# Attention phase of a fused layer kernel: the value product over four query tiles at once, and two output tiles before a batch's last half

## The chip, the cores and the metric

The kernel runs on one core of a Trainium2 chip. The metric is the device time of one execution in microseconds. All data is float32.

## What is computed

The reference is two transformer-like layers one after the other: a state-space block with a top-2 mixture of experts, then causal attention with a second mixture of experts. The change touches only the attention of the second layer:

```python
qkv = jnp.einsum('bte,fe->btf', x, Wqkv).reshape(B, T, H, 3 * D)
q, k, v = ...                       # each B, H, T, D
q, k = q + pe, k + pe
scores = jnp.einsum('bhtd,bhsd->bhts', q, k) / sqrt(D)
probs = softmax(where(causal, scores, -inf), axis=-1)
attn = jnp.einsum('bhts,bhsd->bhtd', probs, v)
out = jnp.einsum('btf,ef->bte', attn.reshape(B, T, H * D), Wo)
...
x = x + ga * out
```

Here B = 4 sequences ("batches") of T = 1024 tokens, 8 heads of D = 128, model width 256. After it the result is normalised again with other modulation rows (`cb`, `sb`), and a router picks two of 16 experts for each token.

## The kernel before

`phase_attention` is one block in which every engine has its own program, and semaphores tie them together. A batch is `HEADS * TPB` = 64 steps, numbered n, for 8 heads h = n // 8 and 8 query tiles i = n % 8 of 128 tokens. For one query tile i only the keys up to it count, that is i + 1 tiles of 128.

**TensorE** does in step n, in this order: `score(n)` (queries stationary, keys moving, up to 1024 columns into one of two score banks), `project` of one of six pieces of the next head's queries, keys and values (in six of the eight steps, `PROJECT`), `turn(n - 2)` (i + 1 transposes of 128x128 of the probabilities of two steps ago into `pt_ps`), and `weigh(n - 3)` (L1794 to L1804). In steps 32, 36, 40 and 44 (`R_PAIR`) `turn_pair` comes ahead of `weigh` and `logits` behind it: router work of the previous batch. Step 52 (`RANK`) has `count_before`, and step 53 waits for the ranks. Steps 56 to 63 (`TURN`) transpose the next batch's normalised rows (`turn_rows`). Behind the loop come eight `output(t)`, 8 matmuls of 256 columns each.

`weigh(n)` is the product with the values: for each key tile j up to i one matmul with the value tile j stationary and one transposed 128x128 block of probabilities moving, i + 1 matmuls of 128 columns, summed in `o_ps`. Each float32 matmul of the source stands as two weight loads and two matmuls in the trace.

**ScalarE** does in step n: `copy_turned(n - 2)` (L1901, out of `pt_ps` into `pt`), then `exponential(n)`; `copy_pair` between the two in the steps of `R_PAIR`, and at step 26 (`ROOT`) the square roots of the norms.

**VectorE** does in step n: `keep(n - 4)` (L2109, a copy of 128x128 out of `o_ps` into `attn`, which waits for `weigh(n - 4)`), then side work, then `maximum(n)` (mask, row maximum, bias), `normalise(n - 1)` (reciprocal and scale, L2101 and L2104), and `take_piece` (L2081, L2085) of the piece projected in the step. Side work is `stats` for the next batch in steps 1, 4, ..., 22 (`ADD`), `variance` at step 24 (once for the next batch and once for the router's norm of the previous; batches 0 and 3 have one of them), route rows in steps 29 to 43, `pick` in 46 and 48, weights, ranks and slots in 52 to 54, and `normalise_rows` of the next batch in 53 to 60. After the loop it adds each output tile to `x` (L2146 to L2150).

So the places that matter in a head are `score` -> `maximum` -> `exponential` -> `normalise` -> `turn` -> `copy_turned` -> `weigh` -> `keep`. `score(n)` waits for `exponential(n - 2)`; `turn(n)` waits for `normalise(n)`.

**SyncE** loads at the start, in this order, the first batch of `x` and `more`, the modulation rows, `mods2` (all modulation rows of the router's norm, 1 MB), `gate_w`, `pos`, `w_o`, then the next batches; it stores the four output batches after its last load. TensorE begins with waits for `w_qkv`, `w_o` and both loads that count in `route_in` (`mods2` and `gate_w`), ahead of its first `turn_rows`.

Of the kernel before, what the change touches and what calls it, by code (L numbers as in the profile page):

```python
# [7 lines left out]
ALU = mybir.AluOpType  # L8
# [1557 lines left out]
def phase_attention(nc, d, sh):  # L1566
# [10 lines left out]
    PIECES = 3 * CPB  # L1577
    with ExitStack() as ctx:
# [12 lines left out]
        pt = sb("pt", [P, 2, TPB, P])  # L1591
# [3 lines left out]
        more = sb("more", [P, TPB, E])  # L1595
# [4 lines left out]
        o_ps = ps("o_ps", [P, P])  # L1600
        qk_ps = ps("qk_ps", [P, CH])
        mods2 = sb("mods2", [P, 2, B, E])
# [11 lines left out]
        names = ("x_in summed route_in stats2_in stats2_chain var2_ready std2_ready rstd2_ready r_half_ready r_row_ready r_turned_done "  # L1614
# [9 lines left out]
        ADD = tuple(1 + 3 * j for j in range(TPB))  # L1624
        VAR, ROOT, INVERT = ADD[-1] + 2, ADD[-1] + 4, ADD[-1] + 6

# [14 lines left out]
        def _(sp):  # L1641
# [8 lines left out]
            sp.dma_start(w_o[:], d["woT"].rearrange("(h p) e -> p h e", p=P)).then_inc(S["w_o_in"], 16)  # L1650
            for b in range(1, B):
# [3 lines left out]
                sp.dma_start(more[:], d["more0"][b * T:(b + 1) * T, :].rearrange("(j p) e -> p j e", p=P)).then_inc(S["x_in"], 16)  # L1655
                sp.wait_ge(S["x_in"], b * 32)
            for b in range(B):
                sp.wait_ge(S["chain"], (b + 1) * TPB)
                rows_out = d["out"][b * T:(b + 1) * T].rearrange("(j p) e -> p j e", p=P)
                sp.dma_start(rows_out, sh.x[:, b * TPB:(b + 1) * TPB]).then_inc(S["x_stored"], 16)  # L1660
# [48 lines left out]
        def _(pe):  # L1709
# [39 lines left out]
            pe.wait_ge(S["route_in"], 32)  # L1749
# [4 lines left out]
            def batch(b, first_batch, last_batch):  # L1754
# [63 lines left out]
                for n in range(N + 3):  # L1818
# [19 lines left out]
                    if n >= 3:  # L1838
                        weigh(n - 3)
# [415 lines left out]
```

## Time and profile before

| | us |
|---|---|
| median of 3 runs | 3036.36 |
| lowest, highest run | 3032.16, 3041.62 |
| the profiled execution's own time | 3031.74 |
| its span, first to last instruction | 3030.0 |
| attention phase, first to last TensorE work | 1478.8 to about 2669 |
| TensorE busy in the span | 2651.9 (88%) |
| VectorE busy in the span | 2219.6 (73%) |

The profile is of one execution. "Busy" of TensorE counts matmuls up to their modelled ends, which overlap: the next matmul starts before the last has ended. Distances from start to start tell how long a stretch of matmuls takes. A span of steps is found by its first `score` of 128 columns (tile 0 of a head).

### The profile page before, as it was taken

How to read it: one execution, taken by the hardware profiler on the slowest of the kernel's cores; microseconds unless marked ns; L12 is line 12 of the kernel's file. 1: busy time of each engine (PE TensorE's matmuls, PEld its weight loads, DVE VectorE, ACT ScalarE, POOL GpSimd, SP SyncE). 2: the span in 40 equal slices, each digit the busy share in tenths (PEclk: the TensorE clock that was granted, in tenths of full speed). 3: DMA queues.
4: the chain of work that ended last, by engine and by line, in shares of the span. 5: the costliest groups of instructions: out<-in, count | busy, mean ns of one | idle time of the engine just before them, and what ended most of it. 6: DMA issues, size and time to landing. Idle time of an engine off the chain costs nothing. (4 is left out here: it accounts for less than half of the span.)

```text
span 3030.0 us, 38485 instructions
## 1 busy us (share of the span) xinstructions
PE 2651.9 (88%) x11504; PEld 1751.7 (58%) x11505; DVE 2219.6 (73%) x4787; ACT 1129.1 (37%) x2199; POOL 1233.9 (41%) x518
## 2 busy tenths in 40 slices
PE   5788888888887859999499999999999999839998
PEld 3233333333333647777277777776777777727776
DVE  4999999999999557777476757766776667525554
ACT  4557566566564201111133414332433233201111
POOL 1798898998999025665100000020002000224444
PEclk8899999999998659999799999999999999959999
DMA  4545545555555343333400000000000000125554
GB/s 156 170 150 181 173 159 178 171 161 175 178 163 177 122 138 60 59 60 58 132 29 1 1 1 29 1 30 15 1 1 29 15 1 1 43 89 126 125 125 71
DMA packets 150092, 269.22 MB, mean 89 GB/s; under 512 B 18300, under 2 KB 106412, under 8 KB 149292
## 3 DMA queue, kind: packets, MB, share of 16 engines
q1 hardware_dynamic: 120972, 227.12, 23.5%
q0 software_dynamic: 28416, 38.05, 7.6%
q10 hardware_dynamic: 544, 2.10, 0.2%
q8 instruction: 80, 1.31, 0.2%
q14 instruction: 80, 0.66, 0.1%
HBM read 209.65 MB, written 57.56 MB: 88 GB/s over the span
## 5 line engine op out<-in xcount | busy, mean ns | idle before, releaser
L692 POOL TENSOR_TENSOR dbx<-u,b_all 128x2048 f32<-128x2048 f32 x128 | 577.8, 4528 | 104.2 <-DVE u L766 49.6
L1690 POOL DMA_INDIRECT slots<-at_r_rows,slot_of x64 | 63.8, 997 | 1170.9 <-DVE slot_of L2035 1152.6
L432 PE MATMUL y_ps<-hc,ident 128*128 128x512 f32 x768 | 406.2, 647 | 115.9 <-DVE hc L846 114.8
L585 ACT ACTIVATE da_ps<-delta,a_neg 128x512 f32<-128x512 f32 x512 | 346.2, 689 | 319.1 <-DVE hc L846 312.7
L1901 ACT COPY at_pt<-at_pt_ps 128x512 f32<-128x512 f32 (+3 forms) x384 | 171.4, 481 | 512.3 <-PE at_pt_ps L1791 511.1
L432 PEld LDWEIGHTS y_ps<-hc,ident 128*128 128x128 f32 x768 | 140.4, 199 | 341.4 <-DVE hc L846 242.6
L1803 PE MATMUL at_o_ps<-at_pt,at_v 128*128 128x128 f32 x2304 | 299.8, 275 | 1.9 <-DVE at_attn L2109 1.9
L1780 PE MATMUL at_s_ps<-at_qk 128*128 128x512 f32 (+3 forms) x768 | 291.4, 489 | 5.0 <-DVE at_v L2085 3.1
L1803 PEld LDWEIGHTS at_o_ps<-at_pt,at_v 128*128 128x128 f32 x2304 | 277.9, 192 | 9.7 <-issue 9.7
L1891 ACT ACTIVATE at_probs<-at_s_ps,at_small 128x128 f32<-128x128 f32 (+7 forms) x256 | 191.6, 748 | 207.3 <-DVE at_small L2096 206.9
L846 DVE TENSOR_TENSOR hc<-da_ps,c_all 128x512 f32<-128x512 f32 x384 | 257.2, 671 | 0.1
L829 DVE TENSOR_TENSOR_SCAN da_ps<-da_ps,state,dbx 128x512 f32<-128x512 f32 x192 | 243.2, 1276 | 6.7 <-ACT da_ps L585 6.7
L829 DVE TENSOR_TENSOR_SCAN da_ps<-da_ps,dbx 128x512 f32<-128x512 f32 x192 | 234.0, 1219 | 3.8 <-ACT da_ps L585 3.8
L1764 PE MATMUL at_qk_ps<-at_h_b,w_qkv 128*128 128x512 f32 x448 | 212.7, 597 | 10.8 <-DVE at_rank L2021 7.8
L1441 POOL DMA_INDIRECT out<-e_ys,e_row_i x80 | 124.8, 1560 | 193.1 <-DVE e_ys L1550 164.1
L2094 DVE TENSOR_REDUCE at_small<-at_s_ps 128x1 f32<-128x128 f32 (+7 forms) x256 | 194.0, 758 | 8.8
L1791 PEld LDWEIGHTS at_pt_ps<-ident,at_probs 128*128 128x128 f32 x1152 | 136.6, 141 | 67.7 <-issue 51.1
L1791 PE MATMUL at_pt_ps<-ident,at_probs 128*128 128x128 f32 x1152 | 169.0, 274 | 7.5 <-DVE at_probs L2104 7.5
L1780 PEld LDWEIGHTS at_s_ps<-at_qk 128*128 128x128 f32 x768 | 126.3, 191 | 70.8 <-issue 63.3
L387 PE MATMUL proj_ps<-h_in,w_in 128*128 128x512 f32 x256 | 134.4, 652 | 34.6 <-DVE x_conv L758 18.6
L2109 DVE COPY at_attn<-at_o_ps 128x128 f32<-128x128 f32 x256 | 73.6, 288 | 122.0 <-PE at_o_ps L1803 120.6
L1475 PE MATMUL e_y_ps<-e_w,e_hid 128*128 128x256 f32 x640 | 152.3, 382 | 5.6 <-ACT e_hid L1498 5.6
(316 smaller groups left out, 4788.0 us busy)
## 6 DMA issues: line engine op xcount, KB each, us to landing
b_all<-bc_rows SPq DMA_DIRECT2D x128, 512.0 KB, 4.5
c_all<-bc_rows SPq DMA_DIRECT2D x128, 512.0 KB, 4.8
e_w<-L_ffn_w SPq DMA_DIRECT2D x32, 512.0 KB, 5.4
slots<-zeros SPq DMA_DIRECT2D x40, 260.0 KB, 6.2
e_xs<-slots SPq DMA_DIRECT2D x16, 650.0 KB, 7.0
w<-L_ffn_W SPq DMA_DIRECT2D x24, 384.0 KB, 8.9
more<-zeros SPq DMA_DIRECT2D x16, 256.0 KB, 4.6
sums<-x SPq DMA_DIRECT2D x8, 512.0 KB, 7.0
```

Of the source, the lines that this page charges most:

```text
L432: mm = nc.tensor.matmul(y_ps[par][:], sh.ident[:], hc[:, at % RING_H, :], start=False, stop=last)
L585: nc.scalar.activation(da_ps[s % RING_DA][:], delta[:, c % 2, m, :], ACT.Exp, scale=sh.a_neg[:, m, n:n + 1]).then_inc(S["da_ready"], 1)
L692: nc.gpsimd.tensor_tensor(dbx[:, at % RING_DBX], pair, rows, ALU.mult).then_inc(S["dbx_ready"], 1)
L829: nc.vector.tensor_tensor_scan(out, h, dbx[:, at % RING_DBX, i // 2, par, :], 0.0 if c % CPB == 0 else state[:, s:s + 1], ALU.mult, ALU.ad ...
L846: nc.vector.tensor_tensor(hc[:, v % RING_H, :], da_ps[s % RING_DA][:], c_all[:, at % RING_C, s % GS // 2, :], ALU.mult).then_inc(S["hc_rea ...
L1764: last = nc.tensor.matmul(out, w_qkv[:, k, h, i // 2, :], h_b[:, i % 2, k, :], start=(k == 0), stop=(k == KE - 1))
L1780: last = nc.tensor.matmul(s_ps[n % 2][:, part * CH:end], qk[:, h % 2, 0, i * P:(i + 1) * P], qk[:, h % 2, 1, part * CH:end], start=True, s ...
L1791: last = nc.tensor.transpose(pt_ps[half][:, j % CT, :], probs[:, n % 3, j * P:(j + 1) * P], sh.ident[:])
L1803: last = nc.tensor.matmul(o_ps[:], v[:, h % 2, j, :], pt[:, n % 2, j, :], start=(j == 0), stop=(j == i))
L1891: nc.scalar.activation(probs[:, n % 3, 0:(i + 1) * P], s_ps[n % 2][:, 0:(i + 1) * P], ACT.Exp, bias=small[:, n % 4, 1:2], scale=SCALE, acc ...
L1901: nc.scalar.copy(pt[:, n % 2, half * CT:half * CT + m, :], pt_ps[half][:, 0:m, :]).then_inc(S[f"copied{half}"], 1)
L2094: nc.vector.reduce_max(small[:, n % 4, 0:1], s_ps[n % 2][:, 0:(i + 1) * P], AX_X).then_inc(S["max_taken"], 1)
```

## The change

- The transposed probabilities go into two buffers, `pt[0]` for query tiles 0 to 3 of a head (4 key tiles by 512 columns) and `pt[1]` for tiles 4 to 7 (8 key tiles by 512 columns). `weigh(h, half, j)` takes the value tile j stationary and up to 512 columns moving, from the first query tile that sees key tile j. In the loop, half 0 is weighed in steps 8h + 6 to 8h + 9 (one j in each), half 1 in steps 8h + 10 to 8h + 13 (two j in each).
- `keep(h, half)` copies 128x512, twice for a head, in the steps with n % 4 == 2. `copy_turned` has the same copies as before, and waits for the older half only at the first tile of a half.
- At the end of a batch, `output(0)` and `output(1)` go ahead of the last half of head 7; its eight matmuls follow at once, and then outputs 2 to 7.
- `mods2` is gone. Its rows are loaded batch by batch into `sh.mods` once that batch's rows are normalised; `more` lies in the last two heads of `attn`, so its load for batches 2 and 3 waits until the outputs of the batch that used `attn` are done. Output stores go out between the loads. `stats` moves to steps 4, 6, ..., 18.

```diff
-        ADD = tuple(1 + 3 * j for j in range(TPB))
+        ADD = tuple(4 + 2 * j for j in range(TPB))
...
-            sp.dma_start(mods2[:], d["mod_rows"][1, 3:5].partition_broadcast(P)).then_inc(S["route_in"], 16)
-            sp.dma_start(gate_w[:], d["gate_wT"].rearrange("(k p) n -> p k n", p=P)).then_inc(S["route_in"], 16)
+            sp.dma_start(gate_w[:], d["gate_wT"].rearrange("(k p) n -> p k n", p=P)).then_inc(S["gate_in"], 16)
...
                 sp.wait_ge(S["summed"], b * TPB)
-                sp.dma_start(more[:], d["more0"][b * T:(b + 1) * T, :].rearrange("(j p) e -> p j e", p=P)).then_inc(S["x_in"], 16)
+                if b > 1:
+                    sp.wait_ge(S["out_done"], (b - 1) * TPB)
+                sp.dma_start(more, d["more0"][b * T:(b + 1) * T, :].rearrange("(j p) e -> p j e", p=P)).then_inc(S["x_in"], 16)
...
-                def weigh(n):
-                    h, i = n // TPB, n % TPB
-                    pe.wait_ge(S["copied0"], b * N + n + 2)
-                    if i >= CT:
-                        pe.wait_ge(S["copied1"], b * (N // 2) + h * CT + i - CT + 2)
-                    pe.wait_ge(S["attn_ready"], b * N + n + 1)
-                    if i == 0:
-                        pe.wait_ge(S["qk_ready"], b * (HEADS * PIECES) + (h + 1) * PIECES + 1)
-                    for j in range(i + 1):
-                        last = nc.tensor.matmul(o_ps[:], v[:, h % 2, j, :], pt[:, n % 2, j, :], start=(j == 0), stop=(j == i))
-                    last.then_inc(S["pv_done"], 1)
+                def weigh(h, half, j):
+                    done = b * (2 * HEADS) + 2 * h + half
+                    if j == 0:
+                        pe.wait_ge(S["attn_ready"], done + 1)
+                        pe.wait_ge(S["copied0"], b * N + h * TPB + (half + 1) * CT + 1)
...
+                    first = max(j - half * CT, 0) * P
+                    last = nc.tensor.matmul(o_ps[:, first:], v[:, h % 2, j, :], pt[half][:, j, first:], start=(j == 0), stop=(j == (half + 1) * CT - 1))
...
-                    if n >= 3:
-                        weigh(n - 3)
+                    if n >= CT + 2:
+                        h, step = (n - CT - 2) // TPB, (n - CT - 2) % TPB
+                        if step < CT:
+                            weigh(h, 0, step)
+                        elif n < N + 2:
+                            weigh(h, 1, 2 * (step - CT))
+                            weigh(h, 1, 2 * (step - CT) + 1)
...
-                pe.wait_ge(S["attn_ready"], b * N + N + 1)
-                for t in range(TPB):
+                for t in range(EARLY_OUT):
+                    if t == 0:
+                        pe.wait_ge(S["exp_done"], b * N + N - 1)
+                        pe.wait_ge(S["attn_ready"], b * (2 * HEADS) + 2 * HEADS)
+                    output(t)
+                for j in range(TPB):
+                    weigh(HEADS - 1, 1, j)
+                for t in range(EARLY_OUT, TPB):
...
-                def keep(n):
-                    h, i = n // TPB, n % TPB
-                    dve.wait_ge(S["pv_done"], b * N + n + 2)
-                    nc.vector.tensor_copy(attn[:, h, i * P:(i + 1) * P], o_ps[:]).then_inc(S["attn_ready"], 1)
+                def keep(h, half):
+                    dve.wait_ge(S["pv_done"], b * (2 * HEADS) + 2 * h + half + 2)
+                    nc.vector.tensor_copy(attn[:, h, half * CH:(half + 1) * CH], o_ps[:]).then_inc(S["attn_ready"], 1)
```

How the instructions stand in a row. TensorE, batch 0, head 0, step 6 to step 9 (`at_s_ps<-at_qk` is `score`, `at_pt_ps` is `turn`, `at_o_ps` is `weigh`, `at_h_b` with `w_qkv` is `project`), before and then after:

```order
698 L1780 MATMUL at_s_ps<-at_qk 128x512
699 L1780 MATMUL at_s_ps<-at_qk 128x384
700 L1769 MATMUL at_qk_ps<-w_qkv,at_h_b 128x128 x8
701 L1791 MATMUL at_pt_ps<-ident,at_probs 128x128 x5
702 L1803 MATMUL at_o_ps<-at_pt,at_v 128x128 x4
703 L1780 MATMUL at_s_ps<-at_qk 128x512 x2
704 L1769 MATMUL at_qk_ps<-w_qkv,at_h_b 128x128 x8
705 L1791 MATMUL at_pt_ps<-ident,at_probs 128x128 x6
706 L1803 MATMUL at_o_ps<-at_pt,at_v 128x128 x5
707 L1780 MATMUL at_s_ps<-at_qk 128x128
708 L1791 MATMUL at_pt_ps<-ident,at_probs 128x128 x7
709 L1803 MATMUL at_o_ps<-at_pt,at_v 128x128 x6
```

```order
695 L1794 MATMUL at_s_ps<-at_qk 128x512
696 L1794 MATMUL at_s_ps<-at_qk 128x384
697 L1783 MATMUL at_qk_ps<-w_qkv,at_h_b 128x128 x8
698 L1805 MATMUL at_pt_ps<-ident,at_probs 128x128 x5
699 L1818 MATMUL at_o_ps<-at_pt,at_v 128x512
700 L1794 MATMUL at_s_ps<-at_qk 128x512 x2
701 L1783 MATMUL at_qk_ps<-w_qkv,at_h_b 128x128 x8
702 L1805 MATMUL at_pt_ps<-ident,at_probs 128x128 x6
703 L1818 MATMUL at_o_ps<-at_pt,at_v 128x384
704 L1794 MATMUL at_s_ps<-at_qk 128x128
705 L1805 MATMUL at_pt_ps<-ident,at_probs 128x128 x7
706 L1818 MATMUL at_o_ps<-at_pt,at_v 128x256
```

The work between one head's last `score` and the next head's first `turn` has become shorter, and it is made up two steps later.

TensorE, end of batch 0, from the transposes of the last two tiles to the outputs (`at_w_o`), before and then after:

```order
940 L1791 MATMUL at_pt_ps<-ident,at_probs 128x128 x7
941 L1803 MATMUL at_o_ps<-at_pt,at_v 128x128 x6
942 L1791 MATMUL at_pt_ps<-ident,at_probs 128x128 x8
943 L1803 MATMUL at_o_ps<-at_pt,at_v 128x128 x15
944 L1810 MATMUL at_s_ps<-at_w_o,at_attn 128x256 x64
```

```order
951 L1805 MATMUL at_pt_ps<-ident,at_probs 128x128 x7
952 L1818 MATMUL at_o_ps<-at_pt,at_v 128x256
953 L1805 MATMUL at_pt_ps<-ident,at_probs 128x128 x8
954 L1818 MATMUL at_o_ps<-at_pt,at_v 128x128
955 L1826 MATMUL at_s_ps<-at_w_o,at_attn 128x256 x16
956 L1818 MATMUL at_o_ps<-at_pt,at_v 128x512 x5
957 L1818 MATMUL at_o_ps<-at_pt,at_v 128x384
958 L1818 MATMUL at_o_ps<-at_pt,at_v 128x256
959 L1818 MATMUL at_o_ps<-at_pt,at_v 128x128
960 L1826 MATMUL at_s_ps<-at_w_o,at_attn 128x256 x48
```

Sixteen of the 64 output matmuls now stand ahead of the last eight of the value product.

VectorE, step 48 of batches 1 and 2, where the second `pick` begins (L1999 before, L2032 after), before and then after:

```order
2504 L2085 COPY at_v<-at_qk_ps 128x512
2505 L2109 COPY at_attn<-at_o_ps 128x128
2506 L1999 TENSOR_REDUCE at_top<-at_scores 128x8
2507 L1986 REGISTER_ALU
2508 L2000 TENSOR_TENSOR at_cand<-at_scores,at_top 128x128
```

```order
2436 L2117 COPY at_v<-at_qk_ps 128x512
2437 L2032 TENSOR_REDUCE at_top<-at_scores 128x8
2438 L2019 REGISTER_ALU
2439 L2033 TENSOR_TENSOR at_cand<-at_scores,at_top 128x128
```

The copy out of `o_ps`, with its wait for TensorE, no longer stands ahead of the side work.

## Rows read from the trace of the kernel before

**Rows 1.** The page, busy time of each engine: share of the span, instructions.

```profile
PE 2651.9 (88%) x11504; PEld 1751.7 (58%) x11505; DVE 2219.6 (73%) x4787; ACT 1129.1 (37%) x2199; POOL 1233.9 (41%) x518
```

**Rows 2.** Window of one head of batch 1; busy us (count), granted clock, DMA share, GB/s.

```profile
1835.58:1865.75 30.17, 30.17 (x183) 22.65 (x182) 22.16 (x60) 11.41 (x29) 0.00 (x0) 1.00 0.20 66
```

**Rows 3.** Groups by form, attention: count, busy us, mean ns, idle before.

```profile
L1803 PE MATMUL at_o_ps<-at_pt,at_v 128*128 128x128 f32 x2304 | 299.8, 275 | 1.9 <-DVE at_attn L2109 1.9
L1803 PEld LDWEIGHTS at_o_ps<-at_pt,at_v 128*128 128x128 f32 x2304 | 277.9, 192 | 9.7 <-issue 9.7
```

**Rows 4.** Timeline of TensorE, batch 0: start, length, work of each run.

```profile
1502.55 1.88 PE L1764 MATMUL at_qk_ps<-at_h_b,w_qkv 128*128 128x512 f32 x4
1504.27 0.81 PE L1780 MATMUL at_s_ps<-at_qk 128*128 128x384 f32 x2
...
1527.81 1.50 PE L1803 MATMUL at_o_ps<-at_pt,at_v 128*128 128x128 f32 x12
1529.15 0.60 PE L1780 MATMUL at_s_ps<-at_qk 128*128 128x256 f32 x2
```

**Rows 5.** Waits of TensorE in the attention: total us, times, longest.

```profile
PE at_qk_ps L1764 <- DVE at_rank L2021: 7.8, 3, 2.7
PE at_pt_ps L1791 <- DVE at_probs L2104: 7.5, 14, 1.1
...
PE at_qk_ps L1769 <- DVE at_v L2085: 4.3, 3, 2.1
...
PE at_s_ps L1780 <- ACT at_probs L1891: 1.9, 4, 0.5
```

**Rows 6.** Start of the attention: two timeline rows, a window, loads (KB, us to landing).

```profile
1473.77 0.48 DVE L2060 SCALAR_TENSOR_TENSOR at_rows<-at_rows,rstd,mods 128x256 f32<-128x256 f32 x1
...
1478.84 0.66 PE L1723 MATMUL at_qk_ps<-ident,at_rows 128*128 128x128 f32 x2 [30.04 <-DMA at_w_o<-woT]
...
1470.00:1475.00 5.00, 0.00 (x0) 0.00 (x0) 4.26 (x15) 0.21 (x1) 0.00 (x0) 0.50 1.02 394
...
at_mods<-mod_rows SPq DMA_DIRECT2D x1, 1024.0 KB, 11.7
...
at_more<-more SPq DMA_DIRECT2D x2, 1024.0 KB, 5.6
```

**Rows 7.** Timeline, batch 1, steps 24 and 25: the variance and the turn behind.

```profile
1865.95 0.29 DVE L2109 COPY at_attn<-at_o_ps 128x128 f32<-128x128 f32 x1 [0.42 <-PE at_o_ps L1803]
...
1871.51 1.09 PE L1791 MATMUL at_pt_ps<-ident,at_probs 128*128 128x128 f32 x8 [1.13 <-DVE at_probs L2104]
```

**Rows 8.** Timeline, batch 1, steps 32 and 36: the router's pair.

```profile
1896.49 0.69 DVE L2104 TENSOR_SCALAR at_probs<-at_probs,at_small 128x896 f32<-128x896 f32 x1
...
1898.22 0.93 PE L1791 MATMUL at_pt_ps<-ident,at_probs 128*128 128x128 f32 x7
...
1899.71 0.60 ACT L1865 COPY at_gated<-at_qk_ps 128x512 f32<-128x512 f32 x1
...
1900.76 0.96 PE L1738 MATMUL at_qk_ps<-at_gate_w,at_gated 128*128 128x16 f32 x8
...
1916.23 1.07 PE L1738 MATMUL at_qk_ps<-at_gate_w,at_gated 128*128 128x16 f32 x8 [0.23 <-ACT at_gated L1865]
```

**Rows 9.** Batch 1, steps 53 and 55, and the window with the clock.

```profile
1985.65 1.98 PE L1764 MATMUL at_qk_ps<-at_h_b,w_qkv 128*128 128x512 f32 x4 [2.67 <-DVE at_rank L2021]
...
1997.25 3.68 PE L1769 MATMUL at_qk_ps<-w_qkv,at_h_b 128*128 128x128 f32 x16 [2.06 <-DVE at_v L2085]
...
1995.00:2000.00 5.00, 2.94 (x14) 2.75 (x14) 4.74 (x12) 1.10 (x2) 4.05 (x4) 0.74 0.30 107
```

**Rows 10.** Timeline, end of batch 0, and a copy of 128x512.

```profile
1732.53 0.98 PE L1791 MATMUL at_pt_ps<-ident,at_probs 128*128 128x128 f32 x7 [0.64 <-DVE at_probs L2104]
...
1740.17 22.07 PE L1810 MATMUL at_s_ps<-at_w_o,at_attn 128*128 128x256 f32 x101 [0.38 <-DVE at_attn L2109]
...
1859.70 0.68 DVE L2085 COPY at_v<-at_qk_ps 128x512 f32<-128x512 f32 x1
```

More of the change, by code:

```diff
@@ L1590, in phase_attention @@
         probs = sb("probs", [P, 3, T])
-        pt = sb("pt", [P, 2, TPB, P])
+        pt = [sb(f"pt{half}", [P, CT * (half + 1), CH]) for half in range(2)]
         attn = sb("attn", [P, HEADS, T])
@@ L1594, in phase_attention @@
         gated = sb("gated", [P, 2, E])
-        more = sb("more", [P, TPB, E])
+        more = attn[:, HEADS - 2:, :].rearrange("p h (j e) -> p (h j) e", e=E)
         r_turned = gated[:].rearrange("p j (k t) -> p j k t", k=KE)
@@ L1599, in phase_attention @@
         pt_ps = [ps(f"pt_ps{i}", [P, CT, P]) for i in range(2)]
-        o_ps = ps("o_ps", [P, P])
+        o_ps = ps("o_ps", [P, CH])
         qk_ps = ps("qk_ps", [P, CH])
-        mods2 = sb("mods2", [P, 2, B, E])
         r_rows = sb("r_rows", [P, TPB, ROW])
@@ L1654, in _ @@
                 sp.wait_ge(S["summed"], b * TPB)
-                sp.dma_start(more[:], d["more0"][b * T:(b + 1) * T, :].rearrange("(j p) e -> p j e", p=P)).then_inc(S["x_in"], 16)
+                if b > 1:
+                    sp.wait_ge(S["out_done"], (b - 1) * TPB)
+                sp.dma_start(more, d["more0"][b * T:(b + 1) * T, :].rearrange("(j p) e -> p j e", p=P)).then_inc(S["x_in"], 16)
                 sp.wait_ge(S["x_in"], b * 32)
[L1657 to L1660, printed above, removed]
+                load_route_mods(b - 1)
+                if b > 1:
+                    store_out(b - 2)
+            load_route_mods(B - 1)
+            store_out(B - 2)
+            store_out(B - 1)
             sp.wait_ge(S["x_stored"], 16 * B)
@@ L1817, in batch @@
                     project(0, i)
-                for n in range(N + 3):
+                for n in range(N + 2):
                     if n < N:
@@ L1898, in copy_turned @@
                         act.wait_ge(S[f"turned{half}"], (b * N + n + 1) if half == 0 else (b * (N // 2) + n // TPB * CT + i - CT + 1))
-                        if n >= 2 and half == 0:
-                            act.wait_ge(S["pv_done"], b * N + n)
-                        nc.scalar.copy(pt[:, n % 2, half * CT:half * CT + m, :], pt_ps[half][:, 0:m, :]).then_inc(S[f"copied{half}"], 1)
+                        if n >= TPB and i % CT == 0 and half == 0:
+                            act.wait_ge(S["pv_done"], b * (2 * HEADS) + n // CT)
+                        at = slice(i % CT * P, (i % CT + 1) * P)
+                        nc.scalar.copy(pt[i // CT][:, half * CT:half * CT + m, at], pt_ps[half][:, 0:m, :]).then_inc(S[f"copied{half}"], 1)
                 for n in range(N + 2):
@@ L2104, in normalise @@
                     nc.vector.tensor_scalar(row, row, small[:, n % 4, 3:4], None, ALU.mult).then_inc(S["normed"], 1)
[L2106 to L2109 removed]
+                def keep(h, half):
+                    dve.wait_ge(S["pv_done"], b * (2 * HEADS) + 2 * h + half + 2)
+                    nc.vector.tensor_copy(attn[:, h, half * CH:(half + 1) * CH], o_ps[:]).then_inc(S["attn_ready"], 1)
                 for i in range(PIECES):
                     take_piece(0, i)
[L2113 to L2115 removed]
+                for n in range(N + 3):
+                    if n >= 2 * CT + 2 and n % CT == 2:
+                        keep((n - 2 * CT - 2) // TPB, n // CT % 2)
                     if not last_batch:
@@ L2144, in batch @@
                     tile = b * TPB + t
+                    if t == EARLY_OUT:
+                        keep(HEADS - 1, 1)
                     dve.wait_ge(S["out_done"], tile + 1)
```

37 lines of the change are left out of this document (27 added, 10 removed).

## The prediction

> **What bounds the kernel now.** I read the busy shares first: TensorE is busy 88% of the span, VectorE 73% [rows 1]. The change lies in the attention only, so I then cut that phase into heads. A head of batch 1 without side work lasts 30.17 us, and TensorE is busy for all of it at the full clock, VectorE for 22.16 us [rows 2]. So a head is worth what TensorE's instructions are worth, and the question is how fast they stream.
>
> Start-to-start distances give that. Four matmuls of 512 columns take 1504.27 - 1502.55 = 1.72 us, 0.430 each. Twelve of 128 columns, each with its own weight load, take 1529.15 - 1527.81 = 1.34 us, 0.1117 each; four of them are 0.447. The time goes by columns, and a weight load beside each narrow matmul hides almost wholly [rows 4]. The row of 12 lasts 1.50 us but holds the engine 1.34, so a wait that the profile shows as w costs about w + 0.16.
>
> Third I read the waits. Beside the start they are few, and most stand where VectorE is late, with the router's ranks, the scaled probabilities or the value pieces: 7.8, 7.5 and 4.3 us over the phase [rows 5].
>
> **The product itself.** Before, a head has 36 products of 128 columns, 72 matmul instructions (2304 in all for 32 heads, [rows 3]): 72 x 0.1117 = 8.04 us. After, half 0 has widths 512, 384, 256, 128 and half 1 has five of 512 and then 384, 256, 128. That is the same number of columns (4608) in 24 instructions: 12 x 0.430 + 4 x (0.323 + 0.215 + 0.112) = 7.76 us, the widths between interpolated. The gain is 0.28 to 0.29 us a head, **9.2 us** over 32. Bounds: 7 us if a wide one costs 4 x 0.1117 less only 4 ns for each instruction saved, 10 us if the narrow ones are at 0.112 to 0.113.
>
> **The copies out of o_ps.** 256 copies of 0.288 us become 64 of about 0.68, the length of another 128x512 copy out of PSUM [rows 10]. VectorE sheds some 30 us, worth nothing where TensorE is the bound. What counts is that `keep` also was a wait for TensorE at the head of each step; it is now there in one step of four.
>
> **The start.** TensorE's first transpose waits until `w_o` lands, at 1478.84. The rows it needs were there from 1474.25 (1473.77 + 0.48). The DMA runs at 394 GB/s meanwhile, and the 1024 KB of `mods2` are ahead of `w_o` on the queue [rows 6]: 1.05 MB / 394 GB/s = 2.7 us less. Some of the projection behind it runs at the granted clock of 0.5, and the clock may rise at the same moment as before, which would give half of it back; I take **2.2 us**, between 1.3 and 3.0. The loads that replace `mods2` are 256 KB each and wait for nothing that is late. The load of `more` for batches 2 and 3 now goes out after the outputs; the first projection (10.5 us by the spacings above) and four steps lie before `stats` needs it, and such a load took 5.6 us [rows 6]. Both and the stores: nothing. If that cover were gone, `stats` at step 4 would hold VectorE and then `turn` for the rest of the load.
>
> **What moves within a head.** By the spacings above I added up TensorE's work for each step. The new `weigh` takes 0.86, 0.64, 0.43, 0.21 us in steps 6, 7, 0, 1 of a head and 1.7, 1.7, 1.5, 0.64 in steps 2 to 5; the old one 0.89, 1.11, 1.33, 1.55 and 1.78, 0.22, 0.44, 0.66. So between the last `score` of a head and the `turn` of its tile 7, two steps on, TensorE has 1.4 us less to do, and between steps 2 and 5 it has 2.5 us more. Where VectorE or ScalarE is just in time the first makes waits and the second takes them away. In a head without side work `turn` of tile 6 had 1.04 us to spare (a step as in [rows 8]: 1898.22 against 1896.49 + 0.69); 0.5 remain. Tile 7 has a projection more ahead of it, and more to spare. No new wait there.
>
> Place by place:
> - Step 26, square roots on ScalarE: `score(29)` waited 0.47 in each batch [rows 5]. The 2.5 us of more work in front of it cover that: 4 x 0.63 = **2.5 us gained**.
> - Step 25, behind the variance: `turn(23)` waited 1.13 in batches 1 and 2. It comes 1.4 us earlier, but VectorE no longer has `keep` ahead of the variance, 0.42 of waiting and 0.29 of copying [rows 7]. 2 x 0.68 = **1.4 us lost**. Bounds: nothing, and 2.8.
> - Router pairs at steps 32 and 40: `logits` started at 1900.76, when ScalarE's copy had been done since 1900.31 (1899.71 + 0.60). ScalarE is tied to step 31's score and doesn't move; TensorE would be there 1.4 us earlier, so it waits about 1.0: 6 x 1.0 lost. At steps 36 and 44 `weigh` ahead of `logits` grows from 0.45 to 1.5, and the wait of 0.23 (0.39 with its overlap) goes: 6 x 0.39 gained [rows 8]. Together **3.6 us lost**, between 0 and 6.
> - Steps 52 to 55: VectorE is the bound there, from ahead of 1985 to behind 1997 (waits of 2.67 and 2.06, [rows 9]). It begins that stretch about 1.9 us earlier, since step 51's score comes sooner, and does 0.4 us less of copying; in it the first wait shrinks to about 0.5 and the second grows to about 2.7; and `turn(55)`, which had no wait, gets one of 1.3, less in batches 0 and 3. I get 1.1 to 1.3 for batches 1 to 3, and 0.8 lost in batch 0: **3.0 us gained**, between -2 and 5. The clock fell to half behind the wait of 2.06 (mean 0.74 in that window; 16 narrow matmuls stand as 3.68 us where 16 x 0.1117 is 1.79 [rows 9]); a dip costs 1.7 us and may come or go with such a wait, so this reaches 3.4 further both ways.
> - Steps 56 to 61: about 0.4 us of new waits, 1.0 of old ones gone where half 1 is weighed: **1.0 us gained** (3 batches, a third each), part of the 7.5 us of [rows 5].
> - End of a batch: `turn(62)` waited 0.64, comes 0.5 us sooner, and VectorE doesn't: 0.5 more; `turn(63)` gets 0.2. The waits for the last two copies (1.9 / 4 = 0.48 of [rows 3] and 0.38 of [rows 10], 1.2 with their overlaps) become one for a copy that is 0.4 longer, about 1.0; the two outputs put ahead hide the other. 4 x 0.5 = **2.0 us lost**. Bounds: 1 us gained, if only the copies count, and 4 lost.
>
> **Sum:** -9.2 - 2.2 - 2.5 + 1.4 + 3.6 - 3.0 - 1.0 + 2.0 = -10.9 us. The profiled execution took 3031.74 (span 3030.0), so it would take 3020.8. The median of the three is 4.6 us above it; I take the difference off the median: 3036.36 - 10.9 = **3025.5**.
>
> **Rivals.** (1) *The waits eat it.* TensorE reaches each just-in-time point sooner and stands there. If the bad end of the step 25, router, ranks and batch-end terms holds (2.8 + 6 + 2 + 4 = 14.8 in place of 1.4 + 3.6 - 3.0 + 2.0 = 4.0), the gain is about 0: 3036. For it speaks that VectorE and ScalarE pieces don't get shorter; against it, that a plain head has slack at every point I could compute. (2) *The single accumulator.* `o_ps` is one bank, and half 1 can't start before `keep` of half 0 is through VectorE's queue, nor the next half 0 before `keep` of half 1. In a plain head the copy is through 1.0 us after the half's last matmul, and TensorE comes back after a score, a projection and a transpose, 2.5 us; VectorE may be 1.4 us late before it shows. From an exposed wait of 0.17 us on each of the 64 copies the gain is gone, from 0.31 on the kernel is measurably slower; at 0.5 each, 32 us come on top: 3057. The waits of VectorE on `o_ps` before (it was idle, not late) speak against. (3) *Loading weights is what costs.* The weight loads of L1803 are 277.9 us busy of 299.8 [rows 3]; if each removed pair of load and matmul were worth its whole 0.1117 us, 1536 of them give 172 us: 2865. Rows 4 speak against it, by 0.430 for four times the columns.
>
> The Trainium skill, TensorE: Matmul & The Clock Gate, section Back-to-back issue gap, gives for streams of load and matmul about 81 ns at 128 columns and 131 ns at 512. By that four narrow ones cost 2.5 times a wide one, and this change would be a large gain of the kind of rival 3; the trace has 1.04 times (0.447 against 0.430, float32), and the measurement decides.
>
> **Chances.** The sum about as worked out, 9 to 20 us faster: 0.50. More, up to 28, where the router and end terms cost nothing and dips go: 0.08. Rival 1, within 9 us either way: 0.33. Rival 2, slower: 0.07. Rival 3: 0.02. A measurement tells 0.3%, 9.1 us, from no change. Faster 0.60, same 0.33, slower 0.07. The range takes the first three, and the 4 us by which a median can stray: 3008 to 3038.
>
> **What would show it.** Right: a plain head takes 29.9 us at a TensorE busy all through; line 1818's runs of 512 keep 0.43 spacing; the first transpose comes near 2.7 us sooner after the block's start; no wait of `score(29)`; `logits` at steps 32 and 40 with waits near 0.8, none at 36 and 44; the batch's outputs start behind a wait near 0.8. Wrong: plain heads at 30.2 or more with waits of `weigh` for `at_attn`, or `turn` for `at_probs` in every head; more stretches at half clock than the two before; a head far under 29.9.

## The result

The changed kernel takes 3019.61 us (median of 6 runs, 3018.64 to 3022.82) against 3036.24 for the kernel before (6 runs, 3032.16 to 3041.73). The ratio is 0.9946, with a 95% interval of 0.9934 to 0.9958: faster by 16.6 us, 0.54%. The forecast was 10.9 us faster, 3025.5, in a range of 3008 to 3038.

The page's first part, of the kernel after, answers [rows 1]. TensorE has 1536 instructions less and is busy for only 6 us less, VectorE has 192 less:

```profile
PE 2645.9 (88%) x9968; PEld 1628.0 (54%) x9969; DVE 2200.3 (73%) x4595; ACT 1126.3 (37%) x2199; POOL 1233.9 (41%) x518
```

The next two answer [rows 2] and [rows 4]. First the window of one plain head, that is a head without side work (batch 1, head 2), with the same columns as [rows 2]. Then two runs of TensorE's timeline: four wide matmuls of the value product from 1560.49, and the next score from 1562.21.

```profile
1828.36:1858.28 29.92, 29.92 (x133) 18.77 (x132) 20.66 (x53) 11.30 (x29) 0.00 (x0) 1.00 0.00 1
```

```profile
1560.49 1.88 PE L1818 MATMUL at_o_ps<-at_pt,at_v 128*128 128x512 f32 x4
1562.21 1.02 PE L1794 MATMUL at_s_ps<-at_qk 128*128 128x512 f32 x2
```

The head is 29.92 for 30.17 us, with TensorE busy throughout, and a wide matmul holds it for 1.72 / 4 = 0.430 us. The waits of TensorE from 1500 to 2600 us of the kernel after, which answer [rows 5]:

```profile
PE at_pt_ps L1805 <- DVE at_probs L2136: 9.2, 9, 1.7
PE at_qk_ps L1783 <- DVE at_v L2117: 7.4, 6, 2.5
PE at_qk_ps L1752 <- ACT at_gated L1896: 4.1, 6, 0.7
PE at_s_ps L1826 <- DVE at_attn L2140: 3.3, 4, 0.9
...
PE at_qk_ps L1778 <- DVE at_rank L2054: 0.9, 3, 0.4
```

The wait for the ranks went from 7.8 to 0.9 us, and that of `score` for the square roots (1.9) is gone. Those for scaled probabilities and value pieces have grown. In the same window of the kernel before, the waits for scaled probabilities were 6.7 us (the 7.5 of [rows 5] has the end of batch 3 with it).

The places that the prediction names, in the timeline of TensorE after: the first transpose of the phase; in batch 1 the turn behind the variance, `logits` at step 32, steps 53 and 55, and `turn(55)` in step 57; then the end of batch 0. The row at 1954.86 is step 47 of batch 1, a wait that the prediction doesn't name.

```profile
1478.39 0.66 PE L1737 MATMUL at_qk_ps<-ident,at_rows 128*128 128x128 f32 x2 [27.84 <-DVE at_rows L2093]
...
1863.74 1.10 PE L1805 MATMUL at_pt_ps<-ident,at_probs 128*128 128x128 f32 x8 [1.69 <-DVE at_probs L2136]
...
1892.95 1.06 PE L1752 MATMUL at_qk_ps<-at_gate_w,at_gated 128*128 128x16 f32 x8 [0.68 <-ACT at_gated L1896]
...
1954.86 2.05 PE L1783 MATMUL at_qk_ps<-w_qkv,at_h_b 128*128 128x128 f32 x16 [0.50 <-DVE at_v L2117]
...
1976.55 1.99 PE L1778 MATMUL at_qk_ps<-at_h_b,w_qkv 128*128 128x512 f32 x4 [0.28 <-DVE at_rank L2054]
...
1988.54 3.37 PE L1783 MATMUL at_qk_ps<-w_qkv,at_h_b 128*128 128x128 f32 x16 [2.51 <-DVE at_v L2117]
...
1995.94 1.10 PE L1805 MATMUL at_pt_ps<-ident,at_probs 128*128 128x128 f32 x8 [0.33 <-DVE at_probs L2136]
...
1726.78 0.98 PE L1805 MATMUL at_pt_ps<-ident,at_probs 128*128 128x128 f32 x7 [1.11 <-DVE at_probs L2136]
...
1730.40 4.77 PE L1826 MATMUL at_s_ps<-at_w_o,at_attn 128*128 128x256 f32 x21 [0.88 <-DVE at_attn L2140]
```

The distances between the first scores of the heads tell where the time went. This table is worked out from their starts in the two traces. "Last" runs from the first score of head 7 through the outputs to the next batch's first score (batch 3: to the router's first transposes behind it).

| us | head 0 | 1, 2 | 3 | 4 | 5 | 6 | last |
|---|---|---|---|---|---|---|---|
| batch 0 before | 25.03 | 30.17 | 30.91 | 30.17 | 30.17 | 30.17 | 71.49 |
| after | 22.59 | 29.92 | 29.92 | 29.92 | 29.91 | 29.92 | 72.96 |
| batch 1 before | 25.34 | 30.17 | 32.25 | 33.35 | 33.68 | 37.51 | 71.66 |
| after | 22.59 | 29.92 | 31.98 | 33.51 | 34.28 | 35.32 | 73.02 |
| batch 2 before | 25.33 | 30.17 | 32.26 | 33.35 | 33.68 | 37.17 | 71.97 |
| after | 22.59 | 29.92 | 31.98 | 33.51 | 34.27 | 35.33 | 72.65 |
| batch 3 before | 24.43 | 30.17 | 30.91 | 33.35 | 33.59 | 34.17 | 62.16 |
| after | 22.58 | 29.92 | 29.92 | 33.51 | 34.18 | 32.20 | 64.22 |

Summed by batch the changes are -3.2, -3.6, -3.9 and -2.5 us. Ahead of batch 0, the idle time before the first transpose and the stretch to the first score went from 30.04 + 22.95 to 27.84 + 22.42, -2.7. Together that is 16.0 us for the attention. It is near the 16.6 us between the medians, but the two profiled executions differ by less, 3031.74 against 3018.64 or 13.1 us: the work ahead of the idle time ended 1.8 us later in the trace of the kernel after, and what follows the attention took 1.1 us longer. The change has no edit ahead of the attention; of what lies behind it, only the output stores moved, and no run tests them alone. Part of head 0's gain is only work moved from head 0 to "last": the product begins three steps later in a batch.

### The profile page after: what moved, and what is told of

It reads as the page before. It is cut to its first block and busy times, and to the rows that moved or that the text cites. A ratio compares the mean times of both kernels' runs of the same rounds, so it can differ in the third digit from the quotient of the medians.

```text
span 3016.9 us, 34915 instructions
## 1 busy us (share of the span) xinstructions
PE 2645.9 (88%) x9968; PEld 1628.0 (54%) x9969; DVE 2200.3 (73%) x4595; ACT 1126.3 (37%) x2199; POOL 1233.9 (41%) x518
## 3 DMA queue, kind: packets, MB, share of 16 engines
q8 instruction: 68, 1.11, 0.2%
## 5 line engine op out<-in xcount | busy, mean ns | idle before, releaser
L1818 PE MATMUL at_o_ps<-at_pt,at_v 128*128 128x512 f32 (+3 forms) x768 | 288.5, 487 | 0.0
L2124 DVE TENSOR_TENSOR at_s_ps<-at_s_ps,at_later 128x128 f32<-128x128 f32 x256 | 75.9, 296 | 186.6 <-PE at_s_ps L1794 185.7
L1794 PEld LDWEIGHTS at_s_ps<-at_qk 128*128 128x128 f32 x768 | 137.0, 190 | 126.8 <-issue 94.8
L1818 PEld LDWEIGHTS at_o_ps<-at_pt,at_v 128*128 128x128 f32 x768 | 127.3, 191 | 60.0 <-issue 56.6
```

The lines of the kernel that those rows point to most:

```text
L1794: last = nc.tensor.matmul(s_ps[n % 2][:, part * CH:end], qk[:, h % 2, 0, i * P:(i + 1) * P], qk[:, h % 2, 1, part * CH:end], start=True, s ...
L1818: last = nc.tensor.matmul(o_ps[:, first:], v[:, h % 2, j, :], pt[half][:, j, first:], start=(j == 0), stop=(j == (half + 1) * CT - 1))
```

## The experiments

My theory was the prediction's: TensorE sets the pace, its instructions cost by columns, and the rest are waits at places where VectorE or ScalarE are just in time. The runs of stats_only and keepwait went after what the sum had missed. Each kernel below ran once, except best and best2, and not all ran on the chip of the result. For each, the kernel before ran on the same chip. Where that one took 3074 to 3077 us, "last" of batches 1 to 3 is longer in every kernel (see the end), and I read the other segments. In kernels with the same work there they repeat from chip to chip within 0.05 us, with one exception: head 6 depends on whether the clock falls in it. With the attention of the kernel before, head 6 took 37.51, 37.17 and 34.17 us in batches 1 to 3 of its own profile, and 37.52, 37.52 and 35.82 in that of start_only.

**narrow.** The columns in narrow pieces, at the new places.

```diff
-                    last = nc.tensor.matmul(o_ps[:, first:], v[:, h % 2, j, :], pt[half][:, j, first:], start=(j == 0), stop=(j == (half + 1) * CT - 1))
+                    for at in range(first, CH, P):
+                        last = nc.tensor.matmul(o_ps[:, at:at + P], v[:, h % 2, j, :], pt[half][:, j, at:at + P], start=(j == 0 and at == 0),
+                                                stop=(j == (half + 1) * CT - 1 and at == CH - P))
```

> The changed kernel with each matmul of the value product cut back into pieces of 128 columns (72 instructions a head again), everything else and all places as in the changed kernel. If the width of the moving operand gives the 0.25 us a plain head got shorter (30.17 to 29.92), plain heads are back at 30.17 and the kernel is 8 us slower than the changed one. If it was the placement, plain heads stay at 29.92. The other gains (the ranks, the square roots, the start) come from places and stay in both cases: about 8 us faster than the kernel before.

3062.63 us, where the kernel before took 3073.84 on that chip. The window of head 1 of batch 0:

```profile
1552.40:1582.57 30.17, 30.17 (x183) 22.65 (x182) 20.71 (x53) 11.20 (x29) 0.00 (x0) 1.00 0.01 2
```

The plain head is back at 30.17, to the last digit, with the 183 matmul records of [rows 2]. So the width gives 0.25 us a plain head, 8.0 us if all 32 gave as much. Heads 6 of batches 1 to 3 give only 0.13, 0.01 and 0.16, so the whole is nearer 7.5 (an estimate: "last" can be compared in batch 0 alone, where it gives 0.48). Head 3 of batches 0 and 3 stays without its wait (30.17 for 30.91): that was the placement. The kernel is 11.2 us faster than the one before, where about 8 was expected.

**stats_only.** The kernel before with the later statistics.

```diff
-        ADD = tuple(1 + 3 * j for j in range(TPB))
-        VAR, ROOT, INVERT = ADD[-1] + 2, ADD[-1] + 4, ADD[-1] + 6
+        ADD = tuple(4 + 2 * j for j in range(TPB))
+        VAR, ROOT, INVERT = ADD[-1] + 6, ADD[-1] + 8, ADD[-1] + 10
```

> The kernel before with one edit: the row sums and statistics for the next batch in steps 4, 6, ..., 18 in place of 1, 4, ..., 22. If the statistics at step 1 are what made the second projection of each of batches 0 to 2 wait (0.74, 1.05, 1.04 us), these waits go and head 0 gets 0.9 to 1.2 us shorter in three batches, some 3 us in all. The rival: that wait went because the new value product leaves the first steps of a batch emptier; then it stays here and the kernel is as before.

3071.62 against 3073.84. Head 0 of batches 0 to 2 goes from 25.03, 25.34 and 25.33 to 24.43, the length that batch 3, which has no statistics to take, had before. In TensorE's waits up to 1990 us the row of the kernel before

```profile
PE at_qk_ps L1764 <- DVE at_qk L2081: 1.8, 2, 1.0
```

has no counterpart. So the moved statistics are worth 2.4 us by themselves, without the new product. That they are worth as much in the changed kernel is likely, as its head 0 takes 22.6 us in all four batches; no run has the changed kernel with the old statistics. I had treated that edit as free.

**start_only.** The kernel before with the load of `mods2` out of the way: it goes out behind `w_o`, and TensorE no longer waits for it (the lines of the wait are left out here).

```diff
-            sp.dma_start(mods2[:], d["mod_rows"][1, 3:5].partition_broadcast(P)).then_inc(S["route_in"], 16)
...
             sp.dma_start(w_o[:], d["woT"].rearrange("(h p) e -> p h e", p=P)).then_inc(S["w_o_in"], 16)
+            sp.dma_start(mods2[:], d["mod_rows"][1, 3:5].partition_broadcast(P)).then_inc(S["route_in"], 16)
```

> The kernel before with one edit: the 1 MB load of mods2 goes out behind w_o, and TensorE doesn't wait for it. If the start term is right, TensorE's idle time ahead of its first transpose of the attention goes from 30.0 to about 27.8 us, ended by the normalised rows and not by the load of w_o; all else as before, so about 2.2 us faster. The rival: w_o shares the DMA engines with the loads around it and lands when it did; then nothing changes.

3070.43 against 3073.84. TensorE's first transpose of the phase:

```profile
1479.45 0.66 PE L1723 MATMUL at_qk_ps<-ident,at_rows 128*128 128x128 f32 x2 [28.32 <-DVE at_rows L2060]
```

It begins 1.7 us sooner after the work before it. But the stretch to the first score is 23.85 for 22.95. The windows 1490 to 1495, of this kernel and then of the kernel after, show the granted clock (the first figure behind the busy times) at 0.54 and at 0.93; in the kernel before it is 0.78.

```profile
1490.00:1495.00 5.00, 5.00 (x8) 2.07 (x7) 0.69 (x1) 0.32 (x1) 0.00 (x0) 0.54 0.56 185
```

```profile
1490.00:1495.00 5.00, 5.00 (x12) 2.12 (x11) 1.61 (x3) 0.00 (x0) 0.00 (x0) 0.93 0.13 45
```

So the load is worth 1.7 to 2.2 us of waiting in the two traces, and where the clock rises decides what is left: idle and stretch together were 52.99 before, 52.17 here, 50.26 after, and between 50.1 and 52.2 in the other runs with the changed start.

**keep4.** Four narrow copies for a wide one.

```diff
-                    nc.vector.tensor_copy(attn[:, h, half * CH:(half + 1) * CH], o_ps[:]).then_inc(S["attn_ready"], 1)
+                    for at in range(0, CH, P):
+                        last = nc.vector.tensor_copy(attn[:, h, half * CH + at:half * CH + at + P], o_ps[:, at:at + P])
+                    last.then_inc(S["attn_ready"], 1)
```

> The changed kernel with each copy of 128x512 out of o_ps as four copies of 128x128 with one signal behind the last, some 0.3 to 0.5 us longer in all. If the single accumulator has slack in plain heads, they stay at 29.92; the end of each batch, where the copy is bare, gets 0.3 to 0.5 longer, and step 52 to 56 of batches 1 to 3, where VectorE is the bound, up to 0.5. Together 2 to 4 us slower than the changed kernel. If the accumulator is nearly the bound (the second rival of the prediction), each of 64 copies costs that, 20 to 30 us.

3048.02 on the chip where before took 3073.84. Plain heads stay at 29.92; "last" of batch 0 is 73.31 for 72.96, heads 5 and 6 of batches 1 and 2 34.46 and 35.54 for 34.28 and 35.32. In the segments that can be compared that is 1.6 us in all. The longer copy shows only where it is bare or VectorE is the bound. The single accumulator isn't near the bound, and rival 2 falls.

**early0.** No output ahead of the last half.

```diff
-    EARLY_OUT = 2
+    EARLY_OUT = 0
```

> The changed kernel with no output tile ahead of the last half of head 7: the eight matmuls of half 1 come right behind half 0, then all eight outputs. If the two early outputs hide a wait (for the last transposed tile's copy, or for the last copy out of o_ps), each batch gets longer by it, 0.5 to 1 us, 2 to 4 us in all. By my reading they hide next to nothing: half 1 has to wait for the copy of half 0 just as the outputs did (0.88 us), in which time ScalarE is done with the last tile, and the outputs 0 to 3 that then follow need half 0 only and cover the copy of half 1. Then the last stretch of batch 0 stays within 0.2 us of 72.96.

3019.34 us on a chip where before takes 3032.30. "Last" is 72.89, 73.10, 72.73, 64.17 for 72.96, 73.02, 72.65, 64.22; the wait for the copy has only changed its line:

```profile
PE at_o_ps L1818 <- DVE at_attn L2140: 3.3, 4, 0.9
```

The two outputs ahead are worth nothing that shows (0.07 us and less). They stand in front of a wait that is the same in either order, and the last wait, for the copy of half 1, is covered by outputs 0 to 3 anyway.

**var20.** One of two variances four steps sooner.

```diff
-                        if n == VAR:
+                        if n == VAR - 4:
                             variance(b + 1)
```

> The changed kernel with the variance of the next batch at step 20 in place of 24; the router's variance stays at 24. In batches 1 and 2 both stood at step 24, and the turn of tile 23 waited 1.7 us. Batches 0 and 3 have one variance and no such wait. So head 3 of batches 1 and 2 should go from 31.98 to 29.92, 4.1 us in all, and nothing else should move. The rival, that the square roots on ScalarE make this wait, leaves 31.98.

3018.39 against 3032.30 (one run each; idle and stretch at the start are 1.7 us longer here than in the profile of the kernel after). Head 3 of batches 1 and 2 goes from 31.98 to 30.05, 3.9 us in all, and heads 1, 2, 4 and 5 don't move; "last" of batch 1 is 0.4 longer. The doubled variance was the wait of 1.69. In batch 2 head 6 is 33.70 for 35.33 and "last" 73.85 for 72.65: the clock didn't fall there this time. That gives only 0.4 in all, since `turn(55)` then waits:

```profile
2286.69 1.09 PE L1805 MATMUL at_pt_ps<-ident,at_probs 128*128 128x128 f32 x8 [1.12 <-DVE at_probs L2136]
```

**pairfirst.** The router's pair ahead of the turn, on TensorE and ScalarE.

```diff
-                    if 2 <= n < N + 2:
+                    if 2 <= n < N + 2 and (first_batch or n not in R_PAIR):
                         turn(n - 2)
...
                             turn_pair(b - 1, R_PAIR.index(n))
+                            turn(n - 2)
...
+                    if not first_batch and n in R_PAIR:
+                        copy_pair(b - 1, R_PAIR.index(n))
                     if n >= 2:
                         copy_turned(n - 2)
-                    if not first_batch and n in R_PAIR:
-                        copy_pair(b - 1, R_PAIR.index(n))
```

> The changed kernel with the router's four transposes ahead of the turn of the step, on TensorE, and the copy of the pair ahead of the copies of the turned tile, on ScalarE, in steps 32, 36, 40 and 44. If logits in steps 32 and 40 wait because ScalarE has the tile's two copies and the pair's to do in 1.1 us of TensorE's work, the wait of 0.68 goes and heads 4 and 5 lose about 0.8 us each in three batches, 4 to 5 us in all. If something ahead of it is late (the route rows, or the value piece that frees the bank), the wait only moves to the transposes and the heads stay at 33.51 and 34.28.

3015.34 against 3032.30. The row of `logits` (L1752 for `at_gated`, 4.1 us after) is gone from the waits, heads 4 and 5 are 32.80 and 33.54 for 33.51 and 34.28, 4.5 us in all over three batches. So the order of the pair and the turn was the cause, and no late route row or value piece. The edit changes the order on TensorE and on ScalarE together; which of the two counts isn't separated. The wait of step 47 stays, 0.49 in batches 1 and 2.

**weights50.** Eight small operations out of step 52.

```diff
-        SLOTS = (RANK, RANK + 1, RANK + 2)
+        SLOTS = (RANK - 2, RANK + 1, RANK + 2)
```

> The changed kernel with the eight small operations of weights (1.75 us of VectorE) at step 50 in place of 52. If steps 52 to 56 are bound by VectorE, head 6 of batches 1 to 3 gets shorter by up to 1.7 us (from 35.3 and 32.2), 3 to 5 us in all, mostly in the waits of 2.5 for the value piece. If the clock that falls to half there, or the copies out of o_ps, make the difference, head 6 stays.

3019.20 against 3032.30, and a miss: head 6 is 35.32, 35.33 and 32.13, as before the edit. In step 52 of the kernel after VectorE still waits 0.68 us for the score behind these operations (batch 1), so the 1.75 us there cost nothing. My reading that all of steps 52 to 56 is bound by VectorE was wrong at its beginning.

**norm55.** Two normalised rows out of steps 53 and 54.

```diff
-        NORM, TURN, COPY = N - 11, N - 8, N - 7
+        NORM, TURN, COPY = N - 9, N - 8, N - 7
```

> The changed kernel with the normalised rows of the next batch two steps later (55 to 62 in place of 53 to 60). Moving the eight weight operations out of step 52 changed nothing, so VectorE isn't yet the bound there; if it is bound from the ranks in step 53 to the value piece of step 54, two rows of 0.96 us less in steps 53 and 54 take 1.5 to 1.9 us from the wait of 2.5 at step 55: head 6 of batches 1 and 2 from 35.3 to about 33.6. Batch 3 has no such rows and stays at 32.2. The last stretch may get back 0 to 1 us by rows in steps 61 and 62. If the slots' chain alone holds the piece, head 6 stays.

3058.65 on a chip where before takes 3077.20. Head 6 of batches 1 and 2 is 32.27 and 32.25 for 35.3, and batch 3's stays at 32.21; "last" of batch 0 stays at 72.96. The wait at step 55, 2.51 before the edit:

```profile
1987.66 2.05 PE L1783 MATMUL at_qk_ps<-w_qkv,at_h_b 128*128 128x128 f32 x16 [1.07 <-issue]
```

So VectorE is the bound from the ranks on. The gain of 3.1 a batch is more than the 1.9 us of rows: behind the shorter wait the clock doesn't fall here either (16 matmuls in 2.05 us; 3.37 in the kernel after).

**keepwait.** VectorE waits at the head of each step for the product of TensorE's step before, as `keep` had made it do.

```diff
+                    elif half == 0 or j % 2:
+                        last.then_inc(S["stepped"], 1)
...
+                    if n >= CT + 3:
+                        at, k = divmod(n - CT - 3, TPB)
+                        if k % CT == CT - 1:
+                            dve.wait_ge(S["pv_done"], b * (2 * HEADS) + 2 * at + k // CT + 2)
+                        else:
+                            dve.wait_ge(S["stepped"], b * (6 * HEADS) + 6 * at + 3 * (k // CT) + k % CT + 1)
```

> The changed kernel, in which VectorE again waits at the head of every step for the value product of TensorE's step before, as the copy out of o_ps made it do in the kernel before, but with no more copies than now. If it counts that VectorE is let go, the stretches where it is the bound get longer: head 3 of batches 1 and 2 by 0.3 us, head 6 and the last stretch together by 0.5 to 1 in batches 1 to 3 (the ranks and the end came out 3 us better than forecast in all), 2 to 5 us in all. If the gain of head 6 is from where TensorE's work stands and from VectorE's 30 us less of copying, the segments stay as they are within 0.1.

3065.51 where before takes 3077.20. Plain heads stay at 29.92. Head 3 of batches 1 and 2 is 32.28 for 31.98; head 6 is 36.52, 34.92 and 33.17 (in batch 2 without the fall of the clock, to be held against var20's 33.70), so 1.0 to 1.2 us longer; "last" of batch 0 73.25 for 72.96. The wait for the ranks is 1.14 where it was 0.28:

```profile
1979.06 1.98 PE L1778 MATMUL at_qk_ps<-at_h_b,w_qkv 128*128 128x512 f32 x4 [1.14 <-DVE at_rank L2056]
```

With 0.07 to 0.08 in each of heads 5 that is 4.5 us in the segments that can be compared. So in the changed kernel it is worth some 4.5 us that VectorE doesn't wait at each step, where shedding 30 us of its copies is worth 1.6 in the same segments (keep4). This isn't quite the wait of the kernel before: the product that VectorE waits for now stands at its new places, up to 1.7 us of it in one step, and each wait is an instruction more.

**best** and **best2.** The edits of var20 and pairfirst together; best2 with that of norm55 as well.

> The changed kernel with two of the edits together: the next batch's variance at step 20, and the router's pair ahead of the turn. Each took its own part alone (head 3 of batches 1 and 2 by 1.9 us, heads 4 and 5 of three batches by 0.7 each), at places that don't touch: 3.8 + 4.3 = 8 us below the changed kernel, about 3011 where that has 3019. If one gives the other's gain back, 3 to 5 us only.

> The same two edits and the normalised rows two steps later. If these are worth their 1.5 to 1.9 us in two batches, 3 us below the run with two edits; if the last stretch gives it back, the same.

On a chip where the kernel before takes 3077.20 (7 runs), best takes 3054.61 (4 runs, ratio 0.9925, interval 0.9908 to 0.9942) and best2 3051.88 (4 runs, 0.9921, 0.9905 to 0.9938). Segments: head 3 30.05 in batches 1 and 2, heads 4 and 5 32.8 and 33.55; in best2 head 6 32.27. The edits add up place by place. Against the kernel after, heads 3 to 5 are some 8.3 us shorter in both; heads 6 are another 6.1 shorter in best2, and in best 1.6, in batch 2, where the clock didn't fall. "Last" of batches 1 to 3, which is disturbed on that chip, can't be compared, so part of this may be given back there. Both are faster than the kernel before. Their intervals overlap with each other and with that of the changed kernel (0.9934 to 0.9958), so by run times alone the order of the three isn't settled.

## Why the prediction was right, and where its sizes were off

The forecast held in kind: the product gave what its columns and instructions were said to give, and most of the waits named came and went. That the sum was 5 us short in the attention has two main causes: an edit without a term, and waits near the end of the batches that were sized wrong. One term that fits, that of the router pairs, fits by luck.

| term | forecast | measured |
|---|---|---|
| width of the product | -9.2 | -8.0 |
| start | -2.2 | -2.7 |
| square roots | -2.5 | -3.0 |
| variance | +1.4 | +1.4 |
| router pairs | +3.6 | +3.8 |
| ranks, steps 56 to 61, end | -2.0 | -5.1 |
| statistics at step 1 | none | -2.4 |
| sum | -10.9 | -16.0 |

The measured terms are worked out from the table of heads with 0.25 a head taken out for the width: square roots 4 x (0.99 - 0.25) = 3.0; variance 2 x (0.74 + 0.25 - 0.27) = 1.4; pairs 3 x (0.16 + 0.25 + 0.60 + 0.25) = 3.8. The sixth line is heads 0, 6 and last of all batches (-10.5) less width (3.0) and statistics (2.4). It holds for these two traces: had the clock fallen in head 6 of batch 3 before, as it did in start_only and stats_only (35.82 and 35.85 for 34.17), it would be 1.7 more.

- **The product.** Right in kind: the price is by columns. The 0.28 to 0.29 us a head rested on 0.1117 from one run of twelve; over a whole head the difference is 0.25. The range of 7 to 10 held it, though its lower end was worked out wrong: 4 ns for each of 1536 instructions saved are 6.1 us.
- **The start.** The load of `w_o` landed 2.0 us sooner after its issue, where I had 2.7 (the rows of the loads, before and then after):

```profile
at_w_o<-woT SPq DMA_DIRECT2D x1, 1024.0 KB, 15.0
```

```profile
at_w_o<-woT SPq DMA_DIRECT2D x1, 1024.0 KB, 13.0
```

  It must still be what TensorE waits for: it was issued at 1465.01, so it landed at 1478.0, and the transposes begin at 1478.39, while the first rows were ready at 1476.19. The releaser that the profile names, a row, happened to end at that moment. I had set the clock against it, half of the gain given back. In this profile it gave 0.5 more; in start_only it took 0.9. That term is a draw, 0.8 to 2.9 us.
- **Square roots, variance.** The waits named came and went as said: `score(29)` none, `turn(23)` 1.69 (forecast 1.13 + 0.68).
- **Router pairs.** `logits` waits 0.68 at steps 32 and 40 and not at 36 and 44, as said, but for 0.68 and not 1.0. Head 4, which has only the pairs, lost 0.41 beyond the width; that is 2.5 us for heads 4 and 5 of three batches, where 3.6 was forecast. Head 5 lost 0.44 more: in step 46 the first `pick` now stands behind a copy out of `o_ps` of 0.69 us where it had one of 0.29, and the value piece comes late: the projection of step 47 waits 0.50, 0.49 and 0.40. That wait had no term; its 1.3 us make up for the rest. No run isolates it.
- **The ranks.** The waits of steps 53 and 55 in batch 1 came out as forecast, 0.28 and 2.51 for 0.5 and 2.7. The step that failed is the one behind: `turn(55)` was to wait 1.3 and waits 0.33, since the projection of step 55 ran mostly at the lower clock and held TensorE for 3.37 us. Where the clock stayed up (batch 2 of var20: 2.05 us), `turn(55)` waits 1.12, as forecast. So a fall of the clock there doesn't cost the 1.7 us that I gave it, but about 0.4: most of it stands where TensorE would have waited anyway. Heads 6 got 5.2 us shorter beyond the width, and the new waits of `turn(55)` (0.57, 0.33 and 0.29 in batches 0, 1 and 3) take 1.2 of that back as shown, 1.7 with 0.16 added to each. That leaves 3.5 to 4.0 for a forecast of 3.0.
- **Behind the ranks: steps 56 to 61 and the end.** This is the mis-sized part of the sixth line. 1.0 us lost was forecast for both together, and 1.1 to 1.6 gained is what is left of the -5.1. The old waits of `turn` in steps 60 and 61 were 2.2 us over the four batches, and all are gone, for a forecast gain of 1.0; `turn(63)` was to wait 0.2 in each batch and doesn't. How much of this comes from VectorE being let go isn't settled. The prediction saw that `keep` no longer holds VectorE at each step and gave it no price of its own; keepwait puts it at 4.5 us, 3.4 of them in heads 6, 0.6 in heads 3, 0.3 in "last" of batch 0 and 0.2 in heads 5.
- **The end.** `turn(62)` waits 1.11 and the outputs 0.88 in batch 0, as forecast. That the two early outputs do nothing (early0) agrees with the sum, in which they had no term but "hide the other"; they don't hide even that.
- **What a shown wait costs.** The prediction added 0.16 us to each. The runs don't bear that out as a rule: 0.47 (`score(29)`) cost 0.74, 0.74 and 1.05 (L1764, batches 0 and 1) cost 0.60 and 0.91, and 0.68 (`logits`) cost 0.71.
- **What was missed.** The edit of `ADD` stood in the diff and had no term. The row that it answers (L1764 waiting for `at_qk`, 1.8 us in the first two batches) was among the waits, and I read only the larger ones.
- **Rivals.** Loading weights is not what costs: four narrow ones cost 0.447, one wide 0.430, and narrow shows that in a plain head nothing else hangs on the width. The accumulator has its slack. That the waits eat the gain was true for 5.2 us (variance, pairs and step 47). var20 takes 3.9 and pairfirst 4.5 out of these heads; the wait of step 47 stays.

## What to carry to other kernels

TensorE was busy throughout a plain head, and making its instructions fewer and wider was worth only a fixed cost for each one saved, about 5 ns of 112. Read such a cost from start-to-start distances, not from durations. The other half of this change lay in what moved: add up the bound engine's work between a producer and its consumer for each step before and after, and look where a just-in-time partner will now be late or covered. Give every edit of the diff a term, and every longer operation a look at what is queued behind it. A copy that waits for another engine also holds everything queued behind it; here making it rare was worth more than making it short (4.5 us in keepwait against 1.6 in keep4).

## What the runs showed of the hardware

The clock fell to half behind waits of 2.06 us ([rows 9], before) and 2.51 us (after; 0.66 in the window 1988.5 to 1993.5) in a stretch that is otherwise busy, but not each time. In batch 2 of the kernel before it fell already behind the wait of 2.67 us for the ranks, which in batch 1 it didn't (1.00 in 1985 to 1990); and in batch 2 of var20 a wait of 2.52 us had no fall behind it (1.00 in 2279.5 to 2284.5). The window of the kernel after in batch 1, then that of the kernel before in batch 2:

```profile
1988.50:1993.50 5.00, 4.96 (x26) 4.69 (x27) 4.65 (x10) 0.79 (x3) 3.78 (x5) 0.66 0.25 89
```

```profile
2279.00:2284.00 5.00, 4.21 (x12) 2.54 (x13) 4.12 (x10) 0.40 (x1) 0.00 (x0) 0.67 0.00 0
```

On two of the chips the kernel before takes 3074 to 3077 us, 38 to 41 more than on the chip of the result. The trace of narrow, from such a chip, shows where: in "last" of batches 1 to 3, while GpSimd issues the scatters of the routed rows (16 a batch, 1.3 us apart), TensorE, VectorE and ScalarE stand for microseconds (up to 5.8, 4.4 and 7.4 in batch 1), and for ScalarE's and VectorE's longest wait the profile names no engine that they waited for. On the chip of the result the same scatters stand in the same place, and the profile has no such wait. ScalarE's waits in narrow, from 1990 to 2100:

```profile
ACT at_pt L1935 <- remote: 10.8, 4, 7.4
ACT at_pt L1935 <- issue: 4.4, 1, 4.4
```

"Last" of batch 1 is 85.43 there for 73.43 of batch 0, 83.86 in stats_only; on the chip of the result batches 0 and 1 differ by 0.1. That is some 12 us each in batches 1 and 2 of narrow and 14 to 15 in batch 3, 38 in all. Why those chips do it is open. keep4 had only 6 us each in batches 1 and 2 on the same chip, and 15 in batch 3.
